# A pre-norm attention block and a mixture of experts on one core: middle residual by an adding SBUF transfer, LN1 statistics on ScalarE, two heads of tile 2 from GpSimd to VectorE

## The reference

```python
x = L0_attn_q_x                                   # 16 x 512 x 256
x = x + attn(layernorm(x))
x = x + ffn(layernorm(x))

def attn(q_x):                                    # no attention between tokens: the 16 heads of one token mix
    xn = ln(q_x, ln1_w, ln1_b)
    q, k, v = (xn @ w + b for each).reshape(b, n, 16, 16)
    fq, fk = elu(q) + 1, elu(k) + 1
    kv  = einsum("bhnd,bhne->bnde", fk, v)
    qkv = einsum("bhnd,bnde->bhne", fq, kv)
    qk  = einsum("bhnd,bnd->bhn", fq, fk.sum(heads))
    x = q_x + (qkv / (qk + 1e-6)) @ wo + bo
    h = gelu(ln(x, ln2_w, ln2_b) @ fc_w + fc_b)
    return x + (h @ proj_w + proj_b)

def ffn(x):                                       # 8 experts, the best 2 of each token, and a shared one
    out = sum over chosen experts of weight * (silu(x @ wg.T) * (x @ wu.T)) @ w_down.T
    return (silu(x @ sg_gate.T) * (x @ sg_up.T)) @ sg_down.T + out
```

## Time and profile before

| | us |
|---|---|
| median of 3 runs | 1806.62 (1806.27 to 1808.12) |
| the profiled execution | 1806.18 |
| its span in the profile | 1804.5 |
| busy: TensorE | 1700.4 (94%) |
| busy: GpSimd | 1244.4 (69%) |
| busy: VectorE | 1214.8 (67%) |
| busy: ScalarE | 723.5 (40%) |
| the bodies, up to some | 1195 |
| the expert stage behind them | 609 |

### The profile page before, as it was taken

How to read it: one execution, slowest core, us unless ns; L and a number is a source line. 1 busy time by engine, 2 the same in 40 slices (tenths; PEclk the granted TensorE clock), 3 DMA queues, 4 the chain that set the end, 5 groups by cost and what they waited for, 6 DMA issues and landing times.

```text
span 1804.5 us, 25211 instructions
## 1 busy us (share of the span) xinstructions
PE 1700.4 (94%) x7288; PEld 1236.1 (69%) x7289; DVE 1214.8 (67%) x2292; ACT 723.5 (40%) x1469; POOL 1244.4 (69%) x652
## 2 busy tenths in 40 slices
PE   2588999999999999999999998989999999999997
PEld 1354675665666666666666666658888888888886
DVE  7999999999999999999999986132222222222221
ACT  2244445445455355355354363322323232323232
POOL 5988899999999899898899994223333333333333
PEclk8688999999999999999999999989999999999999
DMA  5101101101101101101101101156777677777774
GB/s 199 43 4 59 48 21 39 60 15 44 56 15 47 47 23 47 47 23 47 47 23 47 47 13 36 36 155 162 167 154 169 151 167 155 168 152 165 156 167 78
DMA packets 87150, 148.79 MB, mean 82 GB/s; under 512 B 8640, under 2 KB 71872, under 8 KB 86720
## 3 DMA queue, kind: packets, MB, share of 16 engines
q1 hardware_dynamic: 60512, 112.58, 20.0%
q0 software_dynamic: 26592, 35.67, 12.0%
HBM read 101.79 MB, written 48.56 MB: 83 GB/s over the span
## 4 chain that ended last, share of the span: by engine, by line
PE 43%; POOL 41%; issue 7%; DVE 7%; DMA 1%; ACT 1%; POOLq 1%; SPq 0%; DVEq 0%; ACTq 0%
POOL prod_pool L488 16%; PE p_b L1473 10%; PE p_b L1484 10%; POOL prod_pool L509 8%; POOL prod_pool L502 7%; PE p_q L1473 7%; POOL rows_sorted L542 5%; PE p_b L1301 4%; PE p_v L1473 3%; PE p_b L1350 2%; POOL sg_g L551 2%; PE p_xT L1460 2%; PE p_b L1416 2%; DVE p_q L893 1%; DVE prod L884 1%
## 5 line engine op out<-in xcount | busy, mean ns | idle before, releaser
L596 POOL DMA_INDIRECT out_rows<-prod_pool,prod x142 | 220.7, 1554 | 384.1 <-ACT prod_pool L790 353.7
L488 POOL TENSOR_TENSOR prod_pool<-prod_pool 128x2048 f32<-128x2048 f32 (+2 forms) x192 | 400.9, 2088 | 15.1
L1350 PE MATMUL p_b<-bT,fc_sb 128*128 128x512 f32 x512 | 230.7, 605 | 1.3 <-ACT bT L726 1.3
L1301 PE MATMUL p_b<-proj_sb,hid 128*128 128x256 f32 x1024 | 231.6, 379 | 0.0
L1301 PEld LDWEIGHTS p_b<-proj_sb,hid 128*128 128x128 f32 x1024 | 189.8, 190 | 29.2 <-issue 0.5
L1473 PE MATMUL p_b<-prod,exp_up 128*128 128x256 f32 x840 | 187.1, 379 | 0.0
L1416 PE MATMUL p_b<-x3T,sgup_sb 128*128 128x512 f32 x384 | 177.3, 601 | 5.4 <-DVEq L968 3.5
L884 DVE TENSOR_TENSOR prod<-p_q,eqk 128x4096 f32<-128x4096 f32 (+1 forms) x48 | 178.3, 3714 | 4.8
L893 DVE TENSOR_REDUCE p_q<-prod 128x128 f32<-128x2048 f32 x64 | 180.7, 2823 | 1.2
L907 DVE TENSOR_TENSOR prod<-p_q,v_dve 128x4096 f32<-128x4096 f32 (+1 forms) x48 | 178.2, 3713 | 1.7
L920 DVE TENSOR_REDUCE qkv<-prod 128x256 f32<-128x4096 f32 (+1 forms) x48 | 178.0, 3709 | 1.7
(11 more groups left out here) (175 smaller groups left out, 2965.4 us busy)
## 6 DMA issues: line engine op xcount, KB each, us to landing
exp_up<-in_experts SPq DMA_DIRECT2D x71, 768.0 KB
prod<-rows_sorted SPq DMA_DIRECT2D x71, 260.0 KB
xin<-in_x SPq DMA_DIRECT2D x16, 512.0 KB, 3.5
xres<-in_x SPq DMA_DIRECT2D x16, 512.0 KB
out_rows<-x SPq DMA_DIRECT2D x16, 512.0 KB, 2.9
exp_dn<-in_experts SPq DMA_DIRECT2D x8, 384.0 KB, 5.6
out_rows<-prod_pool,prod POOLq DMA_INDIRECT x142, 3.8
rows_sorted<-rows SPq DMA_DIRECT2D x2, 1040.0 KB, 7.1
```

The costliest lines, as they stand in the source:

```text
L488: done(g.tensor_tensor(prod_pool[:, at:at + n * w], prod_pool[:, at:at + n * w], prod_pool[:, at + n * w:at + 2 * n * w], ALU.add))
L596: pool.indirect_dma_start(out=out[:, :], out_offset=bass.IndirectOffsetOnAxis(ap=tok_i[j][:, a:a + 1], axis=0), in_=yg[j][:, a * D:(a + 1) ...
L1301: ins = t_.matmul(o, src[:, k, t * P:(t + 1) * P], w[:, k, :], start=k == 0, stop=bias_at is None and k == chunks - 1)
L1350: ins = t_.matmul(bnk[:], fc_sb[:, k, f * P:(f + 1) * P], bT[:, k, :], start=k == 0, stop=k == KC - 1)
```

## The change

Three things change in the bodies; the expert stage stays.

1. The identity products L1304 go. GpSimd issues, right behind `gate_shared`, a transfer that adds `xmid` into `xres` within SBUF (512 KB); it waits for `xres_loaded` and for `ln2_var`, that is for the end of `residual_1`. `residual_2` waits for it (`xsum_ready`) in place of `xres_loaded`, as does ScalarE before it writes the next `xmid`.
2. `ln1_stats` leaves VectorE. ScalarE sums x (Copy with a summed output), takes the mean, sums the squares of x less the mean, and makes both factors by Ln and Exp, where it made the factors alone before. `ln1_scales` on VectorE stays.
3. `POOL_HEADS` goes from 8 to 6: VectorE's four instructions of u = 2 grow from 2048 to 2560 elements a partition, GpSimd's ten of the shared heads shrink to three quarters.

```diff
-POOL_HEADS = 8
+POOL_HEADS = 6
...
+                if stage_b:
+
+                    wait(pool, xres_loaded, 16 * c)
+                    wait(pool, ln2_var, c)
+                    stand_alone(pool)
+                    pool.dma_start(xres[:].rearrange("p t d -> p (t d)"), xmid[:].rearrange("p t d -> p (t d)"),
+                                   accum_op=ALU.add).then_inc(xsum_ready, 16)
...
+            def ln1_scales(b):
+
+                wait(act, xin_loaded, 16 * (b + 1))
+                wait(act, scale_ready, b)
+                for t in range(TPB):
+                    a.activation(act_junk[:, t, :], xin[:, t, :], ACT.Copy, accum_out=sum_a[:, t:t + 1]).then_inc(ln1_sum, 1)
+                act.wait_ge(ln1_sum, TPB * (b + 1))
+                a.activation(mean_a[:], sum_a[:], ACT.Copy, scale=-1.0 / D).then_inc(ln1_mean, 1)
+                act.wait_ge(ln1_mean, b + 1)
+                for t in range(TPB):
+                    a.activation(act_junk[:, t, :], xin[:, t, :], ACT.Square, bias=mean_a[:, t:t + 1],
+                                 accum_out=square_a[:, t:t + 1]).then_inc(ln1_var, 1)
+                act.wait_ge(ln1_var, TPB * (b + 1))
+                a.activation(sq_a[:, 0, :], square_a[:], ACT.Ln, bias=eps_1[:, 0:1], scale=1.0 / D).then_inc(ln1_log, 1)
+                a.activation(sq_a[:, 1, :], square_a[:], ACT.Ln, bias=eps_2[:, 0:1], scale=(1.0 + EPS) / D
+                             ).then_inc(ln1_log, 1)
+                act.wait_ge(ln1_log, 2 * (b + 1))
+                a.activation(rs_a[:, 0:2], sq_a[:], ACT.Exp, scale=-0.5).then_inc(ln1_std, 1)
...
-                    wait(act, proj_psum, 2 * (c - 1))
+                    wait(act, xsum_ready, 16 * (c - 1))
...
-                    wait(act, ln1_var, c + 2)
-                    rsqrt(rs_a[:, 0:2], sq_a[:], ln1_log, ln1_std, c + 2)
+                    ln1_scales(c + 1)
...
-                    wait(dve, xres_loaded, 16 * c)
+                    wait(dve, xsum_ready, 16 * c)
...
-                    if more:
-                        ln1_stats(c + 1)
...
-                    if plus is not None:
-                        t_.matmul(o, ident[:], plus[:, t, :], start=False, stop=False)
...
-                              between=next_x if more else None, per_bank=True, plus=xmid)
+                              between=next_x if more else None, per_bank=True)
```

More of the change, by code:

```diff
@@ L135, in build @@
         eps_1 = sb("eps_1", [P, 1])
+        eps_2 = sb("eps_2", [P, 1])
+        sum_a = sb("sum_a", [P, TPB])
+        mean_a = sb("mean_a", [P, TPB])
+        square_a = sb("square_a", [P, TPB])
+        act_junk = sb("act_junk", [P, TPB, D], BF16)
         neg_1 = sb("neg_1", [P, 1])
@@ L201, in small @@
                     piece(3 * HEADS))
-        mv_a, mv_b, _ = small(1)
+        _, mv_b, _ = small(1)
         den = [small(j)[2] for j in range(2)]
@@ L224, in build @@
         xin_loaded = sem("xin_loaded")
+        ln1_sum = sem("ln1_sum")
+        ln1_mean = sem("ln1_mean")
         ln1_var = sem("ln1_var")
@@ L718, in body @@
                     wait(act, ln2_scale, c)
+                    wait(act, proj_psum, 2 * (c - 1))
                     norm(lambda t: hnorm[:, t, :], lambda t: xmid[:, t, :], rs_b, h_ready)
                 if more:
-                    wait(act, ln1_var, c + 2)
-                    rsqrt(rs_a[:, 0:2], sq_a[:], ln1_log, ln1_std, c + 2)
+                    ln1_scales(c + 1)
                 if stage_b:
@@ L760, in _ @@
             table_exp_ln()
-            wait(act, ln1_var, 1)
-            rsqrt(rs_a[:, 0:2], sq_a[:], ln1_log, ln1_std, 1)
+            ln1_scales(0)
             norm_1(0)
@@ L828, in averages @@
                 done.sync()
[L830 to L838, removed]
             def ln1_scales(b):
                 wait(dve, ln1_std, b + 1)
-                v.scalar_tensor_tensor(rs_a[:, 2:4], mv_a[:, :, 0].unsqueeze(1).to_broadcast([P, 2, TPB]), -1.0,
+                v.scalar_tensor_tensor(rs_a[:, 2:4], mean_a[:].unsqueeze(1).to_broadcast([P, 2, TPB]), 1.0,
                                        rs_a[:, 0:2], ALU.mult, ALU.mult).then_inc(ln1_scale, 1)
@@ L1138, in body @@
                         dve.sem_inc(pq_free, 1)
-            dve.wait_ge(pool_const, 4)
-            ln1_stats(0)
             done(v.memset(neg_1[:], -1.0))
             done(v.memset(eps_1[:], EPS))
+            done(v.memset(eps_2[:], EPS * EPS))
             announce(dve, v.memset(act_tmp[:], 0.0), tmp_ready, 1)
+            dve.wait_ge(pool_const, 4)
             ln1_scales(0)
@@ L1291, in to_tokens @@
             def to_tokens(src, chunks, w, banks, bias_at, ready, at_last_chunk=None, between=None,
-                          per_bank=False, plus=None, tiles=range(TPB)):
+                          per_bank=False, tiles=range(TPB)):
                 for t in tiles:
```

1 line of the change is left out of this document (added).

## The result

| | us |
|---|---|
| median of 4 runs | 1882.55 (1878.28 to 1883.16) |
| ratio to the kernel before | 1.0414, 95% interval 1.0396 to 1.0432 |
| the profiled execution, its span | 1878.28, 1876.4 |

The change makes the kernel 76 us slower, more than three times the forecast's 23, and outside its range. The profiled execution is the fastest of the four, so the rows show 71.9 of the 76 (the spans are 1876.4 and 1804.5). All of it arises in the bodies: from the first adding store of the expert stage to the end both executions take 579 us. From VectorE's first residual of c = 3 to that of c = 15, twelve blocks, it is 896.3 - 829.3 = 67.0 us; the bodies ahead of them take 2.7 longer, what lies behind 2.2.

A forecast was written before the change was run, and what follows sets the result against it. GpSimd bounds the kernel at 69.10 us a block; the loop behind it, taken as 68.5, becomes 70.95: +22.2 us over twelve blocks, +22.6 with the ends, on 1806.18 gives 1829 us, range 1803 to 1852.

The forecast's parts named there:

- The bound and the loop: GpSimd sets the pace at 69.10 us a block; behind it a TensorE and VectorE loop of 67.83 us, 1.27 below.
- Heads: Four VectorE instructions of tile 2 grow by 533 ns each, 2.13 us in the loop; GpSimd saves 4.6 us.
- LN1 statistics off VectorE: Between LN2 variance and LN2 scale: removal worth only 0.08 us, as VectorE then waits 1.95 for ScalarE's LN2 factor.
- LN1 statistics on ScalarE: Eight passes with summed output and five small ones on ScalarE take 5.2 us, between 3.6 and 7.4.
- Transfer and identity products: Transfer costs GpSimd 1.3 us to issue and is otherwise hidden; TensorE's freed 1.73 us a block become idle time.
- LN1's factor is then ready ... a wait of 0.2, between 0 and 2.4: Factor ready on ScalarE 7.4 us after the LN2 scale; VectorE asks after 7.2, so waits 0.2 us.
- the sum: Block of the loop: 68.5 + 2.13 - 0.08 + 0.2 + 0.2 = 70.95 us, 1.85 more than 69.10.
- where TensorE's idle time would collect: Ahead of TensorE's fc products: they begin about 1.9 us late, then run slowly; fc sums some 3.5 us late.
- the 0.2 for a late softmax weight: VectorE's wait for softmax weights, late behind the fc sums and ScalarE's gelus: 0.2 us a block, between 0 and 1.
- slow clock at the hold: Rival: TensorE idles where L907 holds it, slow products lengthen the loop to 72.2 us, 1844 in all; chance 0.20.
- its 68.5: Loop length taken for the sum before the change's terms, chosen between 67.8 and 69.1 us.
- its two waits of 0.2: VectorE's waits in the loop for ScalarE's LN1 factor and for the late softmax weights, 0.2 us each.

The follow-up runs named there:

- x9: x1 with the first four rows of shared products made twice on TensorE, the result thrown away, to fill its idle time at the hold: 1823.64 us.
- x1: The change with one input of VectorE's LN1 scales row and second routing weight row put in PSUM, plus a small copy: 1840.92 us.
- x2: The change with only POOL_HEADS put back at 8: 1837.11 us.
- x7: The kernel before with only the adding transfer in place of the identity products: 1827.56 us.

## Why the prediction was wrong

- **The bound and the loop: right.** The loop behind GpSimd's pace (18.12 + 49.71 us) is what came to decide, and GpSimd, now 74.11 - 7.70 = 66.4 us of work (forecast 65.8), waits. The slack of 1.27 us was as small as read: with the heads' 2.13 the loop of 67.83 is 69.96, and x9's block is 70.38.
- **Heads: right.** The four rows take 2.82 us, 0.53 more each, all in the loop.
- **LN1 statistics off VectorE: right.** 379.10 - 373.61 = 5.49 us to the LN2 scale, forecast 5.48; the wait of 1.95 stands in nearly every block.
- **LN1 statistics on ScalarE: right in size.** From 381.27 to 386.08, 4.8 us against 5.2 (the upper bound, 8 x 0.79 + 1.0, is 7.3 and not 7.4). The summed output is a separate read-out of 0.19 us behind each pass:

```profile
381.27 0.40 ACT L667 ACTIVATE act_junk<-xin 128x256 bf16<-128x256 f32 x1
381.58 0.19 ACT L667 ACTIVATION_READ_ACCUMULATOR act_junk<-xin 128x1 f32 x1
...
383.24 0.51 ACT L672 ACTIVATE act_junk<-xin,mean_a 128x256 bf16<-128x256 f32 x1
```

- **Transfer and identity products: right.** The transfer holds GpSimd 378.68 - 377.30 = 1.4 us (forecast 1.3), and it lands 4.6 us after its issue at the median, so it is hidden; the products' time went into the hold.
- **The step that failed: "LN1's factor is then ready ... a wait of 0.2, between 0 and 2.4".** It priced the LN1 scales by ScalarE alone. ScalarE's factor did come in time: 386.08 - 379.10 = 7.0 us after the LN2 scale, where VectorE asks for it after 7.2. But the row itself took 0.15 to 4.50 us, 12.6 more than before in twelve blocks, and the routing weight's row, which the sum put at nothing, 12.8 more. The diff shows the LN1 mean moving from PSUM to SBUF, and the prediction did not ask what a second SBUF input does beside GpSimd. The trace of before had the answer in L1028, which has two such inputs: 0.17 to 1.01 us in its blocks for the same work, with ends where a GpSimd instruction ended. And since all heads were shortened, L1051 now meets the 3.70 us L517 where it met short halvings. The Trainium skill ("SBUF — State Buffer", Who interferes with whom) states this: a VectorE instruction with two SBUF inputs and a GpSimd instruction that reads SBUF exclude each other, and the second waits out the first. The rows agree, 4.45 us for one that came 0.08 us late. Price by x1: 41.6 us by the medians, 36.9 between the profiled executions.
- **The second failed step: where TensorE's idle time would collect.** The forecast put it ahead of fc (1.9 us and a slow run there). That gap is 1.2 to 1.3 us in all twelve blocks and the fc products behind it run at speed, 10.57 us against 10.46; the idle time collected at the hold, and the 0.2 for a late softmax weight became no wait at all. This was the rival "slow clock at the hold", given 0.20; it made short statistics of 3.6 us its condition, and came true with 4.8. Its 1.65 us are the 1.7 measured in x1 between a long and a short rest; in the change itself it is 24.5 / 12 = 2.0. Price by x1 and x9: 17.3 us.

With both taken away, x9's block is 70.38 us where the sum had 70.95, and its time 1823.6 where the forecast had 1829: the sum was sound for what it held. That it came so near is in part luck: its 68.5 and its two waits of 0.2 are each a little high, and x9 has the copy, which the sum had not.

## What to carry to other kernels

When a change moves an operand between PSUM and SBUF, list every VectorE instruction whose inputs then both lie in SBUF, and ask which GpSimd instruction runs beside it; look for small rows of varying length, since this wait hides in the duration and no bracket names it. When a pace setter is relieved, the loop behind takes over with all its small waits, and TensorE's new idle time settles at the wait in that loop, where a halved clock, if it follows, is paid in full. Mend that first; work may then be moved by the head until two bounds meet.

## What was not expected of the hardware

- A VectorE instruction of 0.15 us took up to 4.50 us beside GpSimd (5.27 in x2), and hundredths of a microsecond decided. Twice in the trace of the change, first VectorE's row, then GpSimd's; VectorE came 0.04 us ahead of GpSimd in the first pair and 0.04 behind it in the second:

```profile
836.98 0.15 DVE L865 SCALAR_TENSOR_TENSOR rs_a<-mean_a,rs_a 128x8 f32<-128x8 f32 x1
...
837.02 8.31 POOL L496 TENSOR_TENSOR prod_pool<-prod_pool 128x2048 f32<-128x2048 f32 x3
```

```profile
612.26 4.50 DVE L865 SCALAR_TENSOR_TENSOR rs_a<-mean_a,rs_a 128x8 f32<-128x8 f32 x1
...
612.22 8.28 POOL L496 TENSOR_TENSOR prod_pool<-prod_pool 128x2048 f32<-128x2048 f32 x3
```

- TensorE's clock after a hold followed no simple length of it here: in x1 a hold of 2.37 us was followed by slow products in most blocks and not in others; in x7 one of 2.65 us was followed by a rest of 18.18 us. What decides is left open.
